# x transposed by the host and left unnormalised, the scores in two runs, and new orders of work, in a gated cross-attention and mixture kernel

## The reference

```
x = x + tanh(g_xattn) * attention(layernorm(x), ctx)     # 8 heads of 64
    q = layernorm(x) @ Wq;  k = ctx @ Wk;  v = ctx @ Wv
    softmax(q k^T / 8) @ v, then @ Wo + bo
x = x + tanh(g_ffn) * mixture(layernorm(x))
    # 8 experts, all of them computed: gelu(x @ w1[e] + b1[e]) @ w2[e] + b2[e], summed over e,
    # and scaled for each token by a gate made from a softmax over x @ gate_w
```

## Time and profile before

| | |
|---|---|
| median of 3 runs | 1832.39 us (1831.99 to 1833.58) |
| profiled execution, its own time | 1832.89 us |
| its span in the profile | 1831.1 us |
| PE busy | 1804.0 us, 10360 matmuls |
| DVE busy | 1312.9 us |
| ACT busy | 816.0 us |
| POOL busy | 1182.3 us |
| transferred | 110.38 MB, mean 60 GB/s |

### The profile page before, as it was taken

One profiled execution on the slowest core, in us unless ns is written; L12 is line 12 of the kernel. 1 busy time (PEld: TensorE's weight loads), 2 busy tenths in 40 slices (PEclk: granted clock), 3 DMA queues, 4 the chain that ended last, 5 costly groups with the idle time before them and its releaser, 6 DMA issues.

```text
span 1831.1 us, 33020 instructions
## 1 busy us (share of the span) xinstructions
PE 1804.0 (99%) x10360; PEld 1637.3 (89%) x10360; DVE 1312.9 (72%) x2244; ACT 816.0 (45%) x1574; POOL 1182.3 (65%) x900
## 2 busy tenths in 40 slices
PE   7999999999999999999999999999999999999998
PEld 7999999999999988888888888888888888888887
DVE  6778778787877777666666666587766767666667
ACT  5767676676767843232232323243232323223222
POOL 4625345353534779777777777699777777777743
PEclk9999999999999999999999999999999999999999
DMA  5111102021120222212121211113311121212111
GB/s 173 32 30 55 46 28 57 23 68 39 35 67 4 98 95 76 70 46 69 46 69 47 68 57 57 46 66 114 116 58 60 54 69 46 69 46 69 49 44 52
DMA packets 52060, 110.38 MB, mean 60 GB/s; under 512 B 13209, under 2 KB 25497, under 8 KB 52001
## 3 DMA queue, kind: packets, MB, share of 16 engines
q1 hardware_dynamic: 52000, 109.64, 19.0%
HBM read 98.61 MB, written 11.01 MB: 60 GB/s over the span
## 4 chain that ended last, share of the span: by engine, by line
PE 88%; DVE 5%; issue 4%; POOL 1%; ACT 1%; DMA 0%; DVEq 0%; SPq 0%; POOLq 0%; ACTq 0%
PE bank L774 32%; PE scores L747 28%; PE bank L616 16%; PE bank L710 4%; PE scores L687 4%; PE bank L697 4%; DVE xa L889 1%; POOL ctxT L1412 1%; DVE neg_max L976 1%; PE bank L623 1%; DVE acc L1058 1%; DVE xs L893 1%; DVE h_sum L1041 1%; PE scores L832 0%; DVE probsT L893 0%
## 5 line engine op out<-in xcount | busy, mean ns | idle before, releaser
L774 PE MATMUL bank<-w2s,hs 128*128 128x512 f32 x2688 | 621.1, 389 | 2.7 <-DVE acc L1058 1.6
L774 PEld LDWEIGHTS bank<-w2s,hs 128*128 128x128 f32 x2688 | 504.3, 188 | 106.6 <-DVE acc L1058 2.5
L747 PE MATMUL scores<-xs,w1s 128*128 128x448 f32 x2646 | 549.2, 366 | 5.0 <-DVE h_sum L1041 4.9
L747 PEld LDWEIGHTS scores<-xs,w1s 128*128 128x128 f32 x2646 | 495.8, 188 | 49.8 <-DVE h_sum L1041 7.2
L1041 DVE TENSOR_TENSOR h_sum<-scores,h_sum 128x448 f32<-128x448 f32 x441 | 262.5, 619 | 184.3 <-PE scores L747 183.9
L1058 DVE TENSOR_TENSOR acc<-bank,acc 128x512 f32<-128x512 f32 x434 | 295.8, 687 | 126.2 <-PE bank L774 117.1
L1299 ACT ACTIVATE h_full<-h_sum,b1T 128x448 f32<-128x448 f32 x256 | 170.9, 668 | 300.3 <-DVE h_sum L1041 289.7
L893 DVE TENSOR_TENSOR hs<-h_full,hs 128x448 fp32r<-128x448 f32 x256 | 230.6, 901 | 52.4 <-ACT hs L1300 52.4
L1171 ACT ACTIVATE h_sum<-scores 128x448 f32<-128x448 f32 x63 | 34.3, 545 | 478.5 <-PE scores L747 478.5
L1373 POOL TENSOR_SCALAR probs<-probs,row_inv 112x750 f32<-112x750 f32 x60 | 132.5, 2208 | 170.5 <-DVE row_inv L982 170.5
L1475 POOL CAST w1s<-w_stage 128x768 fp32r<-128x768 f32 x64 | 69.0, 1079 | 173.8 <-PE scores L747 170.9
(11 more groups left out here) (122 smaller groups left out, 2149.1 us busy)
## 6 DMA issues: line engine op xcount, KB each, us to landing
w_stage<-in_L_ffn_w SPq DMA_DIRECT2D x128, 512.0 KB, 3.5
ctx_raw<-in_ctx SPq DMA_DIRECT2D x16, 376.0 KB, 3.2
ctx_raw<-in_ctx SPq DMA_DIRECT2D x14, 374.0 KB, 3.1
xa<-in_x SPq DMA_DIRECT2D x16, 224.0 KB, 2.9
xres<-in_x SPq DMA_DIRECT2D x16, 224.0 KB, 2.6
x_scratch<-xres SPq DMA_DIRECT2D x16, 224.0 KB, 2.3
xt_scratch<-yT SPq DMA_DIRECT2D x16, 224.0 KB, 2.8
x_raw<-xt_scratch SPq DMA_DIRECT2D x4, 896.0 KB, 6.2
```

The source lines that it names most:

```text
L747: mm = pe.matmul(product_bank(g, name)[:, 0:TH], w1s[j % 2][:, s, W_OF[name], kc, :], xs[:, i, m, kc, :], start=n == 0, stop=n == 5)
L774: mm = pe.matmul(bank[:, :], hs[j % 2][:, s, ht, t * P:(t + 1) * P], w2s[j % 2][:, m, ht, :], start=n == 0, stop=n == 5)
```

## The change

x comes in twice: as before, and transposed by the host to [batch, 128, 4, 224]. The transposed x is loaded straight into x_turned (load_xt) and split as it is, neither centred nor scaled; item X becomes one split of 128x896 on ScalarE and VectorE, and TensorE has no part in it. The mean is taken out of Wq instead: in the start VectorE sums Wq over its four row pieces (item I, a reduction of 128x1024 to 128x256), TensorE multiplies the sum by a matrix filled with 1/512 (item J, one plain 32-bit matmul of 256 columns), and VectorE subtracts the result from Wq (J), ahead of Wq's split. This is done for both halves of Wq. The factor 1/sqrt(variance) stands in the exponential: its scale operand is now a column q_scale, and the row maximum is multiplied by it in a new small VectorE instruction. L0 stays, since it gives this factor; A0 goes.

The scores are written as two runs, 376 and 374 columns, with two matmuls each, so that they lie without a gap over the border of two banks. The lists of all engines are new. SyncE loads Wq third, before the transposed x and context half 1.

More of the change, by code:

```diff
@@ L60, in number @@
         return n * KC + (item[2] * 2 + item[3] + 1)
-    if kind in ("X", "O", "Y"):
+    if kind in "OY":
         return n * 2 + (item[2] + 1)
+    if kind == "X":
+        return n + 1
+    if kind == "J":
+        return item[2] + 1
     if kind == "K":
@@ L232, in flamingo_kernel @@
         ps = [st.enter_context(nc.psum_tensor(f"bank{i}", [P, 512], F32)) for i in range(RING)]
-        ps_scores = [st.enter_context(nc.psum_tensor(f"scores{i}", [P, 4, 256], F32)) for i in range(2)]
+        ps_scores = [st.enter_context(nc.psum_tensor(f"scores{i}", [P, 1024], F32)) for i in range(2)]
         with ExitStack() as att:
@@ L352, in flamingo_kernel @@
         block = st.enter_context(nc.Block())
-        mb = [ps_scores[i // 2][:, 2 * (i % 2):2 * (i % 2) + 2, :].rearrange("p a n -> p (a n)") for i in range(4)]
+        mb = [ps_scores[i // 2][:, 512 * (i % 2):512 * (i % 2) + 512] for i in range(4)]
         def product_bank(g, name):
@@ L628, in make @@
                 kind = item[0]
-                if kind in "RMDLAWGUZCNF":
+                if kind in "RMDLAWGUZCNFXI":
                     return
@@ L941, in drain @@
                 dve.wait_ge(hi_out[kind], n)
-                if kind == "X":
-                    cols = slice(item[2] * QT, (item[2] + 1) * QT)
-                    last = sub(xnT[:, 1, :, cols], bank[:, 0:KC * QT].rearrange("p (c k) -> p c k", c=KC),
-                               xnT[:, 0, :, cols])
-                elif kind == "K":
+                if kind == "K":
                     _, _, g, p, half = item
@@ L1188, in hi @@
                         w = {"wk": wk, "wq": wq, "wv": wv}[name]
-                        act.wait_ge(w_loaded[item[2]], 16)
+                        if name == "wq":
+                            act.wait_ge(lo_out["J"], g + 1)
+                        else:
+                            act.wait_ge(w_loaded[item[2]], 16)
                         copy(w[:, 0, :, g * GW:(g + 1) * GW], w_raw[:, item[2]]).then_inc(w_hi, 1)
@@ L1229, in hi @@
                 act.wait_ge(in_psum[kind], n)
-                if kind == "X":
-                    if db:
-                        act.wait_ge(in_psum["Q"], number(("Q", 0, 1, 1), b))
-                    cols = slice(item[2] * QT, (item[2] + 1) * QT)
-                    last = copy(xnT[:, 0, :, cols], bank[:, 0:KC * QT].rearrange("p (c k) -> p c k", c=KC))
-                elif kind == "Y":
+                if kind == "Y":
                     if not (isinstance(b, int) and b + db == 0):
@@ L1427, in handle @@
                         pool.wait_ge(w_lo, len(WEIGHT_PIECES) - len(POOL_PIECES))
-                    pool.wait_ge(w_loaded[item[2]], 16)
+                    if name == "wq":
+                        pool.wait_ge(lo_out["J"], g + 1)
+                    else:
+                        pool.wait_ge(w_loaded[item[2]], 16)
                     pool.tensor_copy(w[:, 0, :, cols], w_raw[:, item[2]]).then_inc(pool_w_hi, 1)
@@ L1542, in _, with n_out @@
             steps(pool, step)
+def n_out(b, qt):
+    return b * 2 + (qt + 1)
 def n_ln(which, b, qt):
@@ L1570 @@
     for name in _INS:
-        a = _np.asarray(inputs[name])
-        if name == "ctx_1024":
+        a = _np.asarray(inputs["x" if name == "x_turned" else name])
+        if name == "x_turned":
+            a = a.reshape(B, NQ, KC, P).transpose(0, 3, 2, 1)
+        elif name == "ctx_1024":
             a = a.reshape(B, NK, KC, P).transpose(0, 3, 2, 1)
```

105 lines of the change are left out of this document (61 added, 44 removed).

## The result

The changed kernel is slower: median 1841.44 us (1838.72 to 1843.19, 7 runs) against 1835.48 (7 runs) of the kernel before timed beside it, ratio 1.0035, 95% interval 1.0024 to 1.0045. Its profiled execution took 1843.19 us with a span of 1841.4, which is 10.3 more than the span before; I had forecast 10.3 less.

The account below looks back on a forecast made before the run. TensorE, busy 99% of the span, was taken as the bound. Savings of 4.4 + 1.9 + 2.0 + 1.0 + 1.0 = 10.3 us brought 1832.9 to 1822.6 us, 0.6% less; 8-in-10 range 1816 to 1831.

Parts of the forecast that it names:

- The longer chain behind each score tile: Maximum to exponential: added product 0.2 us per tile on VectorE, longer exponential on ScalarE, both hidden; taken as 0.
- x off TensorE: Loop: two groups of transpositions per batch, 0.63 us, leave TensorE; 4.4 us saved over seven batches.
- scores: Score tiles: two runs of columns instead of three gain 0.015 us a tile over 128 tiles, 1.9 us; bounds -2.6 to +6.4.
- the wait in the product: Attention product, once per batch: TensorE's wait on probsT, counted 0.45 us, filled by other work; 2.0 us saved, 0 to 3.2.
- The start: Before the first body item (36.69 us): K starts at 11.2 to 11.8; 1.0 us saved, between +2 and -2.5.
- rival C: Start and scores: VectorE holds TensorE in the start and the scores gain nothing; gain 5.4, 1827.5 us; chance 0.08.
- C's sign: First body item at or behind 36.69 us, with TensorE's waits there naming VectorE.
- The second operand of the exponential: ScalarE's exponential: per-row scale lengthens it from 0.888 to 0.98 us, 1.5 us per batch, hidden.
- The seam: Passage to the second half: 0.90 us idle on GpSimd's memset goes, losses 3.1 now against 1.9 or 3; 1.0 us saved.
- Rival E: Score chain: TensorE waits where two tiles of one half lie under 2.8 us apart; slower, 1842 us; chance 0.07.

Follow-up runs that it names:

- max_in_psum: Changed kernel with the negated row maximum written to PSUM, so the two-tensor product has one operand in PSUM and one in SBUF: 1826.03 us, 0.9961.
- old_plus_tt: Kernel before plus, per score tile, the row maximum times a column of ones as a two-tensor product of SBUF operands on VectorE: 1849.43 us, 1.0074.
- no_mult: Changed kernel with the product of row maximum and q_scale left out: 1825.29 us, 0.9951.
- two_runs_alone: Kernel before with the scores in two runs of 376 and 374 columns and nothing else: 1834.38 us, 0.9997.
- ts_plain_exp: Changed kernel with the one-tensor, per-row-operand product, and the exponential's scale a constant 1.0 instead of the q_scale column: 1826.24 us, 0.9955.
- sum_on_pe: Changed kernel with one-tensor product and old last-batch lists (its base), plus Wq's column sum on TensorE, first key projection ahead of J0: 1835.20 us, 1.0006.
- ts_no_centring: Changed kernel with the one-tensor, per-row-operand product, and the centring of Wq left out (no I, no J): 1826.37 us, 0.9954.

## Why the prediction was wrong

**The step that failed: "The longer chain behind each score tile".** I priced the product by "the nearest row is the reciprocal, 112x1, 0.154 us; with its own wait 0.2" and called it hidden, so the sum has it at nothing. The reciprocal reads one tensor, the product two, both in SBUF, and GpSimd works for 65% of the span. The size of an instruction says nothing about how long it is held: with one element per row it lasted up to 1.95 us. From the changed kernel to max_in_psum the span falls by 17.2 us: start 2.6, batch 0 1.9, batch 1 1.0, batches 2 to 6 5.2, last batch 4.8, rest 1.8. That is most of the 20.6 us between forecast and profiled time. By the two ratios (1.0035 and 0.9961) it is an estimated 13.6 us. Part of the last batch's 4.8 came by way of the clock, 0.57 of full speed from 644 to 648 us in the changed kernel and 1.00 over the whole seam (630 to 645) in max_in_psum.

The trace before held the warning, in rows that I did not read. Of two splits by the same line and of nearly one size, the one with an operand in PSUM takes 618 ns, the one with both in SBUF 901:

```profile
L893 DVE TENSOR_TENSOR hs<-h_full,hs 128x448 fp32r<-128x448 f32 x256 | 230.6, 901 | 52.4 <-ACT hs L1300 52.4
...
L893 DVE TENSOR_TENSOR probsT<-bank,probsT 125x448 fp32r<-125x448 f32 x192 | 115.0, 618 | 30.5 <-ACT probsT L1171 29.8
```

Of those 256, 157 take at most 630 ns and 99 more, up to 2266. Of the 99, 79 end 479 to 488 ns after a GpSimd TENSOR_TENSOR, the other 20 end 475 to 481 ns after a CAST. Overlap alone does not tell, since 58 of the short ones overlap with a TENSOR_TENSOR too, but 54 of these began in its last 133 ns. So a split that comes while GpSimd is busy lasts until about 0.48 us after GpSimd's instruction, whatever its start. The 128x7 product shown above, 2.27 us in the same trace, is the same case on a tiny size, and it was on TensorE's path. The Trainium skill (SBUF — State Buffer, Who interferes with whom) says that a VectorE instruction with two SBUF inputs contends with a GpSimd instruction that reads SBUF, and that one with at most one such input, outside the two-port modes, does not. By that rule the product would have been a rival with a place and a price. The runs agree for GpSimd's TENSOR_TENSOR, 31 of 31 products held, against none of 30 with one operand in PSUM, and for its CAST (17 of 17 in old_plus_tt); they don't for its TENSOR_SCALAR, during which 38 products took at most 236 ns.

**x off TensorE, scores, and the wait in the product: right in kind, and the sum partly by luck.** I forecast (4.4 + 2.0 + 1.7) / 7 = 1.16 us per batch in the loop; without the hold it is 79.11 - 77.97 = 1.14. But with the product left out altogether it is 1.35 (no_mult), so the three terms gave some 0.2 more than forecast and the unheld product, which I had at nothing, took as much back. two_runs_alone gives the scores 0.09 per batch against my 0.24, so the others gave more. Of the 0.45 us that I counted for the wait, show 0.28 (0.19 idle and 0.54 against 0.45); what each of the others gave was not measured alone. By the sustained gap of the Trainium skill (TensorE: Matmul & The Clock Gate, Back-to-back issue gap) my estimate for a tile was 0.45 us; the trace shows 0.69.

**The start: half right.** J0 stands at 11.30 and K at 11.93, 0.1 behind the forecast 11.2 to 11.8, and VectorE is nearly full. But the reduction, which I priced at 1.2 us by a split of like size, takes 1.95. It reads with a stride of 256 elements; that this is the reason was not tested. Without the hold the first item starts at 37.39, 0.7 late and not 1.0 early, towards rival C. In the changed kernel it is 39.96, with TensorE waiting for VectorE's queries, which is C's sign, but 2.6 of the 3.3 us are the hold.

**The second operand of the exponential: right,** 977 ns against 0.98 forecast.

**The seam: wrong by 2.2 us without the hold.** The wait on the memset is gone, as foreseen; 0.42 us of the 0.90 are left before that product, and the profile names nothing that ends them. But the last batch takes 77.54, where 1.24 less than 76.55 was forecast. What came late instead is in part what I named: 0.9 us on ScalarE's rounding of x2 (yT), further 0.6 on att_sum, 0.3 on rescaled probabilities, 1.0 on xres ahead of w2 (also there before). The per-row operand accounts for 0.4 of it (ts_plain_exp). The other 1.8 us are not settled. The miss is larger than it looks, since the kernel before loses time to the lower clock there (0.62 from 637 to 641 us) and max_in_psum does not; in it ScalarE is busy for 14.83 and VectorE for 14.36 of the 15 us from 630 on, against 13.87 and 11.60 before.

**Rival E came true in sign and time (1842), not in mechanism.** It had TensorE wait for the exponentials; it never did. The product stood in VectorE's queue ahead of the splits that empty the banks. My own rule, to name what is queued behind a waiting instruction, was applied to the added wait on ScalarE and not to VectorE, since I took the product to be short.

## What to carry to other kernels

Before adding a VectorE instruction, count its SBUF tensor inputs and look at what GpSimd runs in the same stretch: two inputs beside a GpSimd TENSOR_TENSOR or CAST mean that it can be held for the rest of GpSimd's instruction, however small it is. Use the form with a per-row scalar, or keep one operand in PSUM. For the per-row form this is shown at 112x1 alone: at 112x512 (L889 in the kernel before) it takes 546 ns by itself and 1115 to 1120 in the seven cases inside a GpSimd TENSOR_SCALAR. And price the free instruction too: 16 of them per batch cost from 0.35 to 1.15 us, by what stands behind them. In the profile, compare the mean of the same operation with and without a PSUM operand, and read min/median/max before a mean; then ask which bank release stands behind the instruction in its queue.

## What the runs showed of the hardware that was not expected

- A two-tensor VectorE product of 112x1 lasts 158 ns alone and ends 13 to 22 ns after GpSimd's TENSOR_TENSOR where one is running (31 of 31), and 11 to 14 ns after its CAST (17 of 17, old_plus_tt). With one operand in PSUM it lasts 158 ns always; with one tensor and a per-row operand 214; on ScalarE 291.
- A GpSimd TENSOR_SCALAR of 112x750 lengthens that product only to 236 ns at most (38 cases in the changed kernel), but a one-tensor VectorE instruction of 112x512 from 546 to about 1117 ns.
- The same hold on a product of 128x7 (2.27 us against 0.17) is in six of the fourteen traces, near the end, and has TensorE wait 1.9 to 2.0 us each time.
- A VectorE sum of 128x1024 to 128x256, read with a stride of 256 elements, takes 1950 ns; a subtraction over 128x1024, 1218.
- In sum_on_pe TensorE started at 7.51 us, 3.2 earlier than in its base, then had a gap of 2.13 us, and the granted clock fell to its lower level (0.86 from 12 to 24 us); the start came out 2.7 us longer. With a start at 7.74 and a gap of 1.34 us (ts_no_centring) it stayed at 1.00.
